# Eight-part query stack, two queues for the maxima, and fp32 dense experts beside five sparse ones in a two-layer attention and mixture kernel

## Chip, cores and metric

One NeuronCore of a Trainium2 chip. The metric is the device time of one execution in microseconds, median of the runs; lower is better. The kernel of before runs at 333.51 us (three runs, 332.26 to 333.8).

## What is computed

1024 tokens of 128 features pass through two layers, each an attention over a context of 96 features and a mixture of experts, all with a normalisation in front and a residual behind:

```python
x = x + L0_xattn(layernorm(x), ctx)     # one head, 4 batches of 256
x = x + L0_ffn(layernorm(x))            # 64 experts, top 6, plus a shared expert
x = x + L1_xattn(layernorm(x), ctx)     # 16 heads of 8, softmax(q k / sqrt 8) v, Wo
x = x + L1_ffn(layernorm(x))            # the last mixture:
    probs = softmax(xt @ Wr);  topv, topi = top_k(probs, 2);  topv /= sum(topv)
    rank = cumsum(onehot(topi), axis=0);  keep = (rank <= 160) * onehot
    w = einsum('tk,tke->te', topv, keep)
    h = gelu(xt @ W1[e] + b1[e]);  y = h @ W2[e] + b2[e];  out = sum_e w[t,e] * y
```

The last mixture has 8 experts of 512 hidden units and a capacity of 160 tokens for each of the two choices.

## The kernel before

It is written in one program per engine, with semaphores; the order on each engine is the order of the code. The first attention and the first mixture (up to 148 us of the span) stay as they are but for details. Then:

**Query stack.** The queries and keys of the second attention are split into three bf16 parts. Eight products of parts (PARTS_Q, PARTS_K) make up one fp32-like product, so each head has 64 stacked rows (KROWS) and three rows of maxima above them. `queries` (L1692, DVE), `query_parts` (L830, ACT), `query_residual` and `query_last` (DVE) make the parts of a batch; for batches 2 and 3 the DVE steps stand in the slots 0 to 4 of the loop below. `queries_stacked` (L463, the SP queue) writes the three parts to DRAM (parts 0 and 1 in one DMA once both exist, then part 2), waits for both writes and loads them back in three DMAs, rows 0 to 23, 24 to 47 and 48 to 63, all 16 heads. POOL clears the stack's upper half beforehand in `query_zeros` (L623): batch 3, then, after the last expert group, batches 0 to 2.

**Attention loop.** All engines walk SLOTS (L856, L1416, L1858). In slot s, PE makes the scores of maximum m = s (`max_scores`, L922 with ks as its second operand), DVE reduces them to the negated maximum (L1863), and PE makes the transposed scores of exponential e = s - LAG (`exp_scores`), for which ACT takes Exp (L879). LAG is 17. After each eight maxima POOL splits them into three bf16 parts (`maxima_parts`), PE transposes them in slot 8k+10, ACT copies them in slot 8k+11 (L862), and SP sends three rows of each half-batch into the query stack (`maxima_stacked`, L484). `exp_scores` waits for them at every eighth head. The division, output product and residual of each token chunk have fixed slots (TAIL_AT, TAIL_LAST), and so have the normalisation and router of each half of the tokens (STATISTICS to ROUTER_WT): steps 48 to 63 for the first half, 68 to 76 for the second.

**Router.** Logits, subtraction of the maximum (DVE), Exp (ACT), the two largest and their indices (DVE), ranks by matmul (PE), then in `router_weights` the slots of the dispatched rows and the weights as three bf16 parts. POOL's `dispatch_rows` scatters the tokens to DRAM in eight indirect DMAs for each half (L671), SP loads them back expert by expert (`dispatched_rows`, L498), PE transposes them (L1388).

**Last mixture.** Experts 3 to 6 are sparse (320 rows each), experts 0, 1, 2 and 7 dense, in two halves of 512 tokens. QS gives the order: six dense half rounds, four sparse rounds, two dense half rounds, each of four steps (NF). A step is `ffn_hidden(n)`, three fp32r matmuls on weights and inputs split into high and low (`split_weights` on POOL, L661 and L662; `operands` on DVE), Gelu twice on ACT (L903 as fp32r, L907 as fp32), the difference on DVE (L1915), and `ffn_out(n)` two steps later, three fp32r matmuls. Dense results are weighted by a broadcast row and summed into accT (L1806, L1854). Sparse results are biased, transposed (L1399), weighted (L1842) and scattered to DRAM by POOL (`return_rows`, L683), the last expert to a plane of its own.

**End.** SP loads the planes 0 and 1 of returned rows, POOL adds them to x (L711); plane 2 is loaded on two queues and added by DVE (L1940), as are the transposed sums (L1946), and x is stored in three chunks.

## Time and profile before

| | us |
|---|---|
| median of three runs | 333.51 |
| the profiled execution | 332.18 |
| its span | 330.4 |

| engine | busy us | share |
|---|---|---|
| PE matmul | 273.7 | 83% |
| DVE | 227.4 | 69% |
| ACT | 166.6 | 50% |
| POOL | 160.6 | 49% |

A busy time is the time in which the engine had an instruction in it; a matmul's includes the time until its result is written, so consecutive ones overlap and a group of n of them lasts n pitches and one latency. The granted clock is given as a share of 2.4 GHz: 1.00 is the upper of two levels, 0.50 (1.2 GHz) the lower. In an idle note as [2.27 <-DMA big<-q_parts] the engine had nothing to do for 2.27 us ahead of the instruction, and what came last was that DMA.

### The profile page before, as it was taken

Reading aid. Unit: us, or ns where it says so; the run is one execution under the profiler, and the core shown is the slowest. Engines: PE = TensorE matmul, PEld = TensorE weight load, DVE = VectorE, ACT = ScalarE, POOL = GpSimd, SP = SyncE. Lnnn points to the kernel's source line nnn. Section 1 sums busy time; section 2 is a strip of 40 time slices with the busy share of each in tenths; the row PEclk is TensorE's granted clock in tenths of the full one; section 3 lists DMA queues with packets and bytes.
Section 4 is the critical chain, followed back from the end, with each engine's and each line's share of the span. In section 5 each row is a group of like instructions: output and inputs, shape, how many; then the busy total and the mean of one; then the engine's idle time right before and its main releaser. Section 6 shows DMA issues by size and latency. Waiting matters only on the chain.

```text
span 330.4 us, 6098 instructions
## 1 busy us (share of the span) xinstructions
PE 273.7 (83%) x2180; PEld 187.6 (57%) x2180; DVE 227.4 (69%) x575; ACT 166.6 (50%) x323; POOL 160.6 (49%) x184
## 2 busy tenths in 40 slices
PE   1996766788989899987359999999898989899970
PEld 0665435367778778865112545554466667679740
DVE  2467889445675564437488777875648788999793
ACT  1455230342354235533232777778686978678830
POOL 5856373854234419426305433302271079977772
PEclk9999955999999999999755899999999999999995
DMA  6972294348996554230421500002300002500044
GB/s 205 305 258 100 63 189 76 41 40 212 207 195 163 147 149 34 86 107 1 111 66 37 128 18 4 1 3 87 110 15 4 0 21 57 165 0 12 27 139 128
DMA packets 22569, 30.66 MB, mean 93 GB/s; under 512 B 2926, under 2 KB 15135, under 8 KB 22283
## 3 DMA queue, kind: packets, MB, share of 16 engines
q1 hardware_dynamic: 19835, 26.46, 27.9%
q0 software_dynamic: 1920, 2.90, 8.0%
q10 hardware_dynamic: 784, 0.92, 0.9%
q8 instruction: 17, 0.28, 0.3%
q14 instruction: 13, 0.11, 0.1%
HBM read 23.19 MB, written 7.92 MB: 94 GB/s over the span
## 4 chain that ended last, share of the span: by engine, by line
PE 51%; DVE 17%; POOL 9%; issue 9%; DMA 7%; ACT 5%; DVEq 0%; SPq 0%; POOLq 0%; ACTq 0%
PE bank L922 43%; PE bank L1119 3%; POOL ew L616 2%; DVE score L1863 2%; POOL dispatched L671 2%; DMA packc<-in_packc 2%; DMA big<-q_parts 1%; DMA ew<-normalised,slot_token 1%; PE bank L1131 1%; ACT ctxT L796 1%; DMA returned_last<-ctxT,big 1%; POOL rstd L563 1%; POOL returned L683 1%; POOL big L626 1%; DMA ks<-returned_last 1%
## 5 line engine op out<-in xcount | busy, mean ns | idle before, releaser
L922 PE MATMUL bank<-frbuf,splits 128*128 128x512 f32 (+1 forms) x240 | 60.9, 388 | 2.0 <-DVE frbuf L1915 1.7
L616 POOL DMA_INDIRECT ew<-normalised,slot_token x32 | 33.1, 1036 | 43.7 <-DVE slot_token L1633 36.0
L1863 DVE TENSOR_REDUCE score<-bank 128x2 f32<-128x512 f32 x64 | 42.2, 687 | 14.4 <-PE bank L922 13.7
L922 PEld LDWEIGHTS bank<-frbuf,splits 128*128 128x128 f32 x240 | 41.9, 188 | 13.6 <-DVE frbuf L1915 3.9
L879 ACT ACTIVATE pbuf<-bank 128x512 f32<-128x512 f32 x64 | 37.1, 598 | 16.0 <-PE bank L922 15.6
L1915 DVE TENSOR_TENSOR frbuf<-pbuf,frbuf 128x512 fp32r<-128x512 f32 (+1 forms) x48 | 36.6, 775 | 5.6 <-ACT pbuf L907 5.1
L1639 DVE CAST splits<-bank 128x1024 fp32r<-128x1024 bf16 x16 | 19.6, 1223 | 25.8 <-PE bank L922 21.5
L903 ACT ACTIVATE frbuf<-bank,biases 128x512 fp32r<-128x512 f32 (+1 forms) x48 | 30.6, 638 | 11.0 <-PE bank L922 10.1
L922 PE MATMUL bank<-ks,big 128*128 128x256 bf16 x128 | 29.5, 323 | 6.4 <-DVE score L1863 3.7
L922 PE MATMUL bank<-splits,frbuf 128*128 128x512 f32 (+1 forms) x144 | 32.0, 373 | 0.8 <-ACT frbuf L824 0.8
L907 ACT ACTIVATE pbuf<-bank,biases 128x512 f32<-128x512 f32 (+1 forms) x48 | 30.3, 631 | 0.0
L671 POOL DMA_INDIRECT dispatched<-xn,didx x16 | 16.3, 1018 | 27.9 <-DVE xn L1784 23.6
L922 PEld LDWEIGHTS bank<-splits,frbuf 128*128 128x128 f32 x144 | 24.6, 188 | 5.1 <-ACT splits L802 1.0
L922 PE MATMUL bank<-big,ks 128*128 128x256 bf16 x128 | 25.3, 285 | 0.4 <-ACT pbuf L879 0.4
L796 ACT COPY ctxT<-bank 128x512 f32<-128x512 f32 x8 | 4.7, 585 | 41.2 <-PE bank L1069 41.2
L922 PEld LDWEIGHTS bank<-ks,big 128*128 128x128 bf16 x128 | 10.0, 106 | 25.1 <-DVE score L1863 13.3
L662 POOL TENSOR_TENSOR splits<-ew,splits 128x512 fp32r<-128x512 f32 x16 | 22.1, 1382 | 1.3
L646 POOL CAST nmp<-score 128x16 bf16<-128x16 f32 x8 | 1.6, 196 | 40.6 <-DVE score L1863 40.6
L802 ACT CAST splits<-bank 128x1024 fp32r<-128x1024 bf16 x16 | 16.2, 1014 | 6.9 <-PE bank L1119 6.9
L922 PE MATMUL bank<-pbuf,vaug 128*9 128x256 f32 x256 | 19.7, 381 | 0.0
L563 POOL TENSOR_TENSOR rstd<-veps,mhalf 128x4 f32<-128x4 f32 (+1 forms) x10 | 9.4, 944 | 18.6 <-DVE veps L1474 16.3
L922 PE MATMUL bank<-xnT,packa 128*88 128x512 f32 (+2 forms) x28 | 15.7, 685 | 1.5 <-ACT xnT L746 1.4
(222 smaller groups left out, 538.7 us busy)
## 6 DMA issues: line engine op xcount, KB each, us to landing
big<-in_w SPq DMA_DIRECT2D x8, 704.0 KB
ew<-in_ew SPq DMA_DIRECT2D x16, 256.0 KB, 3.5
big<-in_w SPq DMA_DIRECT2D x8, 352.0 KB
ks<-k_parts SPq DMA_DIRECT2D x4, 512.0 KB, 8.1
k_parts<-parts SPq DMA_DIRECT2D x2, 768.0 KB, 3.8
big<-q_parts SPq DMA_DIRECT2D x8, 192.0 KB
returned<-vbuf SPq DMA_DIRECT2D x1, 1024.0 KB, 15.2
ks<-returned SPq DMA_DIRECT2D x4, 256.0 KB, 3.7
```

The lines of the kernel that those rows point to most:

```text
L563: pool.tensor_tensor(out=rstd[:, cs], in0=veps[:, cs], in1=mhalf[:, 0:n], op=ALU.pow).then_inc(ln_rstd, 1)
L616: pool.indirect_dma_start(out=xg[:, g % 2, j, :], out_offset=None, in_=xn_dram, in_offset=bass.IndirectOffsetOnAxis(ap=slot_token[:, g % 3 ...
L662: pool.tensor_tensor(out=low, in0=ew[:, e % RING1, i, :], in1=high.bitcast(F32), op=ALU.subtract).then_inc(split, 1)
L671: pool.indirect_dma_start(out=disp_dram, in_=xn[:, c, :], in_offset=None, out_offset=bass.IndirectOffsetOnAxis(ap=didx[:, c, k:k + 1], axi ...
L802: a.copy(PTs[:, j, :], bank[4][:, :].bitcast(BF16)).then_inc(e_PTa, 1)
L879: a.activation(prob1[:, e % NPROB, :], bank[2 + e % 2][:, :], ACT.Exp).then_inc(a_exp, 1)
L903: a.activation(acth[:, n % NA, 0:w], bank[n % 3][:, 0:w], ACT.Gelu, bias=bias).then_inc(f_hi, 1)
L907: a.activation(act[:, n % 4, 0:w], bank[n % 3][:, 0:w], ACT.Gelu, bias=bias).then_inc(f_act, 1)
L922: return pe.matmul(out_, lhsT, rhs, start=start, stop=stop, skip_group_check=True)
L1639: v.tensor_copy(PTs[:, j, :], bank[3][:, :].bitcast(BF16)).then_inc(e_PTv, 1)
L1863: v.tensor_reduce(nm1[:, c, 2 * hp:2 * hp + 2], bank[m % 2][:, :].rearrange("p (h k) -> p h k", h=2), X, ALU.max, negate=True).then_inc(a_ ...
L1915: v.tensor_tensor(out=actl[:, n % NA, 0:w], in0=act[:, n % 4, 0:w], in1=acth[:, n % NA, 0:w].bitcast(F32), op=ALU.subtract).then_inc(f_lo, 1)
```

## The change

- PARTS_Q and PARTS_K change places, so the rows of one query part lie together: parts 0, 0, 0, 1, 1, 1, 2, 2. Each part is written to DRAM as often as it is used, on its own semaphore, and the stack is loaded in two DMAs (parts 0 and 1, part 2), for batch 0 in four, heads 0 to 7 first.
- Queries of batches 2 and 3: the first step goes to ACT with bias and scale, the two differences to POOL. One of POOL's clears moves ahead.
- Of the maxima's three rows SP sends two and ACT the third. LAG is 15.
- The router's softmax goes: the second weight over the first is e to the power of the difference of the logits, taken on POOL, the first is 1/(1 + that). Slots of rows are computed ahead of weights. The steps of norm and router stand earlier.
- Experts 2 to 6 are sparse, 0, 1 and 7 dense. Dense steps use unsplit fp32 weights and one Gelu, one matmul for hidden and one for out. POOL splits only sparse experts, into a ring of four. LOADS gives the order in which weights are loaded, from within the loop of the maxima.
- The rows dispatched are loaded ahead of the last expert's weights. DVE adds planes 0 and 1 ahead of the last weighted product; weighting and summing of the last halves take turns.

```diff
-PARTS_Q = (0, 1, 2, 0, 1, 2, 0, 1)
-PARTS_K = (0, 0, 0, 1, 1, 1, 2, 2)
+PARTS_Q = (0, 0, 0, 1, 1, 1, 2, 2)
+PARTS_K = (0, 1, 2, 0, 1, 2, 0, 1)
-LAG = 17
+LAG = 15
-TAIL_LAST = {6: dict(zip(TAIL_AT, (65, 65, 66, 66, 67, 67))),
-             7: dict(zip(TAIL_AT, (66, 66, 67, 67, 68, 68)))}
+TAIL_LAST = {6: dict(zip(TAIL_AT, (65, 65, 66, 66, 66.5, 66.5))),
+             7: dict(zip(TAIL_AT, (66, 66, 66.5, 66.5, 67, 67)))}
-STATISTICS, NORMALISE, NORM_T, NORMED, OPERANDS = (48, 68), (49, 70), (54, 70), (54, 70), (54, 71)
-ROUTER_LOGITS, ROUTER_SUB, ROUTER_EXP, ROUTER_CHOICES = (56, 72), (56, 72), (57, 73), (58, 73)
-ROUTER_RANKS, ROUTER_WEIGHTS, ROUTER_T, ROUTER_WT = (60, 74), (60, 75), (63, 76), (63, 76)
+STATISTICS, NORMALISE, NORM_T, NORMED = (48, 67), (49, 67), (52, 69), (52, 69)
+ROUTER_LOGITS, ROUTER_CHOICES, ROUTER_RANKS = (53, 69), (54, 69), (56, 70)
+ROUTER_SLOTS, ROUTER_WEIGHTS, ROUTER_T, ROUTER_WT = (56, 70), (57, 71), (59, 72), (59, 73)
-XT_FIRST, XT_AT, Y_AT, YT_AT, YS_AT = -2, -3, 5, 6, 6
+XT_FIRST, XT_AT, Y_AT, YT_AT, YS_AT = -1, -3, 5, 6, 6
-SPARSE = (3, 4, 5, 6)
+SPARSE = (2, 3, 4, 5, 6)
+LOADS = (2, 3, 4, 5, 0, 1, 6, 7)
+LOAD_AT = {3: 3, 4: 5, 5: 7}
+RINGW, NA = 4, 3
...
+        def maxima_row(queue, k, part):
+
+            queue.dma_start(qs[KROWS + part:KROWS + part + 1, k // 2, k % 2 * 8:k % 2 * 8 + 8, :],
+                            nmT[k % 2][part * 8:(part + 1) * 8, batch(k // 2)]
+                            ).then_inc(nm_in[k % 4], 16)
...
+                for part, done in enumerate((q1_hi, q1_mid, q1_lo)):
+                    sp.wait_ge(done, b + 1)
+                    at, n = PARTS_Q.index(part), PARTS_Q.count(part)
+                    sp.dma_start(qscratch[b, at:at + n].rearrange("i p t -> p i t"),
+                                 view(parts[:, part, batch(b)], (0, n), (1, TB))
+                                 ).then_inc(qd_out[part], 16)
+                for heads, done in (((slice(0, 8), qs_in[0]), (slice(8, NH), qs_in8)) if b == 0
+                                    else ((slice(0, NH), qs_in[b]),)):
+                    for at, end in ((0, low), (low, KROWS)):
+                        for part in range(2) if at == 0 else [2]:
+                            sp.wait_ge(qd_out[part], 16 * (b + 1))
+                        sp.dma_start(qs[at:end, b, heads, :], rows[at:end, heads, :]
+                                     ).then_inc(done, 16)
...
                 sp.wait_ge(a_nmT, k + 1)
-                for part in range(3):
+                for part in range(2):
+                    maxima_row(sp, k, part)
...
+            pool.wait_ge(e_Y, NG - 1)
+            query_zeros(0)
             pool.wait_ge(e_Y, NG)
-            for b in range(3):
-                query_zeros(b)
+            query_zeros(1)
+            query_zeros(2)
...
+            for b in (2, 3):
+                pool.wait_ge(q1_hi, b + 1)
+                pool.wait_ge(q1_res, b)
+                pool.tensor_tensor(out=query_rest(b), in0=qf[:, batch(b)], in1=parts[:, 0, batch(b)],
+                                   op=ALU.subtract).then_inc(q1_res, 1)
...
             for k in range(2 * NB):
                 maxima_parts(k)
-                if k < 2 * RING1:
-                    split_weights(k // 2, k % 2)
-            power(8)
+                if k == 2 * NB - 1:
+                    power(8)
+                    pool.wait_ge(ln_rstd, 9)
+                split_weights(SPARSE[k // 2], k % 2)
+            second_choices(0)
             dispatch_rows(0)
             power(9)
+            second_choices(1)
             dispatch_rows(1)
...
+                    a.wait_ge(a_nmT, k + 1)
+                    maxima_row(a, k, 2)
...
+                if h2 is not None:
+                    mm(o, expert_raw(e, 0)[:, chunk(f)], xnT[:, half(h2)]).then_inc(f_H, 1)
+                    return
...
+                if QS[q][1] is not None:
+                    pe.wait_ge(f_act, n + 1)
+                    mm(o, expert_raw(e, 1)[:, chunk(f)], act[:, n % 4, 0:w], start=(f == 0),
+                       stop=(f == NF - 1)).then_inc(f_Y, 1)
+                    return
...
+            v.wait_ge(x3_sb, NC)
+            for h2 in range(2):
+                returned_sum(h2, range(2))
             for at in (0, TB):
                 weighted(NQ - 1, at, TB)
-            for at in (0, TB):
                 summed(NQ - 1, at, TB)
-            returned_sum(0)
+            returned_sum(0, [2])
             layer_sum(0)
-            returned_sum(1)
+            returned_sum(1, [2])
             layer_sum(1)
             layer_sum(2)
```

## Rows read from the trace of the kernel before

**Rows 1.** First line of the profile page: the span.

```profile
span 330.4 us, 6098 instructions
```

**Rows 2.** Windows: us, busy of each engine (instructions), granted clock, DMA share, GB/s.

```profile
166.00:185.00 19.00, 15.28 (x63) 5.61 (x62) 16.60 (x29) 7.18 (x14) 5.28 (x12) 0.51 0.31 68
...
240.00:285.00 45.00, 41.33 (x216) 28.99 (x209) 35.15 (x91) 35.81 (x58) 24.66 (x23) 1.00 0.13 33
285.00:305.00 20.00, 19.22 (x116) 16.51 (x117) 19.30 (x38) 15.16 (x34) 15.73 (x15) 1.00 0.11 39
...
319.00:330.40 11.40, 1.85 (x8) 0.91 (x8) 5.84 (x9) 0.00 (x0) 5.17 (x4) 0.59 0.44 134
```

**Rows 3.** Timeline (start, us, engine, line), matmuls of 512 and 320 columns, one subtraction.

```profile
15.36 1.95 PE L922 MATMUL bank<-xnT,packa 128*128 128x512 f32 x4 [0.38 <-ACT xnT L746]
...
42.77 3.69 PE L922 MATMUL bank<-xnT,packa 128*88 128x512 f32 x4
...
273.73 5.73 PE L922 MATMUL bank<-frbuf,splits 128*128 128x512 f32 x24
...
300.32 0.49 DVE L1915 TENSOR_TENSOR frbuf<-pbuf,frbuf 128x320 fp32r<-128x320 f32 x1
...
300.65 0.60 PE L922 MATMUL bank<-xsT,splits 128*128 128x320 f32 x3
...
301.09 0.60 PE L922 MATMUL bank<-frbuf,splits 128*128 128x320 f32 x3
```

**Rows 4.** Groups by line and shape: count, busy us, mean ns, idle before.

```profile
L1915 DVE TENSOR_TENSOR frbuf<-pbuf,frbuf 128x320 fp32r<-128x320 f32 x16 | 12.3, 782 | 0.1
```

**Rows 5.** Timeline, from the first mixture to the first scores.

```profile
146.94 5.31 POOL L626 MEMSET big<- 64x2048 f32 x3 [11.14 <-PE bank L922]
...
160.03 1.11 SPq L475 DMA_DIRECT2D big<-q_parts  x3
...
165.72 1.01 PE L922 MATMUL bank<-ks,big 128*128 128x256 bf16 x4 [2.27 <-DMA big<-q_parts]
```

**Rows 6.** Timeline of the attention loop's slots.

```profile
166.34 0.69 DVE L1863 TENSOR_REDUCE score<-bank 128x2 f32<-128x512 f32 x1 [4.99 <-PE bank L922]
...
171.13 4.87 DVE L1863 TENSOR_REDUCE score<-bank 128x2 f32<-128x512 f32 x7
...
175.63 0.36 ACT L862 COPY ctxT<-bank 24x256 bf16<-24x256 bf16 x1 [4.24 <-PE bank L1230]
...
176.06 2.20 SPq L484 DMA_DIRECT2D big<-ctxT  x3
...
180.10 0.63 PE L922 MATMUL bank<-big,ks 128*128 128x256 bf16 x2
...
221.60 1.28 DVE L1863 TENSOR_REDUCE score<-bank 128x2 f32<-128x512 f32 x2
```

**Rows 7.** Timeline, from the first half's router to the first sparse step.

```profile
237.64 0.34 PE L1315 MATMUL bank<-identb,wparts 128*24 128x128 bf16 x3 [1.16 <-DVE wparts L1794]
...
238.79 0.93 PE L922 MATMUL bank<-frbuf,splits 128*128 128x512 f32 x3 [0.32 <-ACT ra L873]
...
257.47 1.28 ACT L869 ACT_TABLE_LOAD   x1
...
258.76 0.23 ACT L869 ACTIVATE sres<-sres 128x32 f32<-128x32 f32 x1
...
264.98 1.05 POOL L671 DMA_INDIRECT dispatched<-xn,didx  x1 [13.50 <-DVE xn L1784]
...
276.77 0.38 SPq L498 DMA_DIRECT2D big<-dispatched  x1
...
284.88 0.68 PE L922 MATMUL bank<-xsT,splits 128*128 128x320 f32 x3 [0.84 <-issue]
```

**Rows 8.** The chain of work that ended last (start, us, what), its last hops.

```profile
317.60 4.04 DMA returned_last<-ctxT,big
321.65 3.45 DMA ks<-returned_last
325.20 0.70 DVE x L1940
```

More of the change, by code:

```diff
@@ L430, in _ @@
                 sp.wait_ge(done, 2)
-                at, n = PARTS_K.index(part), PARTS_K.count(part)
-                sp.dma_start(kscratch[at:at + n].rearrange("i p t -> p i t"),
+                n = PARTS_K.count(part)
+                sp.dma_start(kscratch[part:NCOMB:3].rearrange("i p t -> p i t"),
                              view(parts[:, part, :], (0, n), (1, T))).then_inc(kd_out, 16)
@@ L641, in _ @@
                                op=ALU.add).then_inc(x2_sb, 1)
+            pool.wait_ge(x2_sb, NB + 1)
+            for b in (2, 3):
[3 more added lines that the diff above has]
+                                   op=ALU.subtract).then_inc(q1_res, 1)
+                pool.wait_ge(q1_mid, b + 1)
+                pool.wait_ge(q1_lo, b)
+                pool.tensor_tensor(out=parts[:, 2, batch(b)], in0=query_rest(b),
+                                   in1=parts[:, 1, batch(b)], op=ALU.subtract).then_inc(q1_lo, 1)
             def maxima_parts(k):
@@ L847, in _ @@
             norm_transposed(7)
+            for b in (2, 3):
+                a.wait_ge(q1_ps, b + 1)
+                a.wait_ge(q1_f, b)
+                a.activation(qf[:, batch(b)], bank[6 + b % 2][:, 0:TB], ACT.Identity,
+                             bias=bq1s[:, 0:1], scale=SCALE1).then_inc(q1_f, 1)
             query_parts(2)
@@ L1424, in _ @@
                 n = e - TILE0
[L1425 to L1436 removed]
+                for at in (e - 0.5, e):
+                    if at == e and 0 <= n < NT:
+                        ffn_hidden(n)
+                    for name in ("output", "normed transposes", "transposes"):
+                        c = tail_chunk(name, at)
+                        if c is not None:
+                            tail_steps[name](c)
+                    for h2 in range(2):
+                        if at == NORM_T[h2]:
+                            norm_transposes(8 + h2)
+                        if at == ROUTER_LOGITS[h2]:
+                            router_logits(h2)
+                        if at == ROUTER_RANKS[h2]:
+                            router_ranks(h2)
+                        if at == ROUTER_T[h2]:
+                            router_transposes(h2)
                 for hg in range(4 * NB):
@@ L1738, in router_less_maximum @@
                 v.wait_ge(r_ps, h2 + 1)
[L1739 to L1746 removed]
+                chained(v.tensor_copy(rp[:, cs, :], logits))
                 for c in range(first, first + 4):
```

316 lines of the change are left out of this document (141 added, 175 removed).

## Prediction

> **What bounds the kernel now.** Read the span first: 330.4 us [rows 1]; the execution took 332.18 us, so 1.8 us lie around the span, and it is 1.3 us under the median of 333.51. Then read busy time by stage [rows 2]. From 166 to 185 us the attention loop starts at a granted clock of 0.51 (the 1.2 GHz level) and DVE is busy 16.6 of 19 us. From 240 to 285 PE is busy 41.3 of 45 us, though 24 dense steps fill less (below). From 285 to 305 DVE (19.3 of 20) and PE (19.2) are level. In the last 11.4 us PE works 1.85 us: a pure chain of latencies. So PE sets most of the time, but four places wait: the start of the loop, the two routers, the sparse steps with their DVE subtractions, the end.
>
> **The dense mixture steps, removed and added.** Before, a dense step is six fp32r matmuls (three hidden, three out). 24 of them took 5.73 us; with some 0.25 us of latency off, 0.228 each, 1.37 us per step. After, it is two fp32 matmuls on unsplit weights. In the trace one fp32 matmul of 512 columns is two records: the two query projections are four records in 1.95 us, so 0.86 each with the latency off, 1.72 per step at 2.4 GHz; the same form at 1.2 GHz took 3.69 [rows 3]. Sparse steps keep six matmuls of 320 columns; groups of three start 0.44 us apart, 0.88 per step. Before 32 dense and 16 sparse steps: 43.8 + 14.1 = 57.9 us. After 24 and 20: 41.3 + 17.6 = 58.9. **PE work rises by 1.0 us.** What falls is elsewhere: one Gelu instead of two and no DVE subtraction in each dense step, no split of experts 0, 1 and 7 on POOL. The subtractions of 320 columns averaged 782 ns [rows 4], though the one at 300.32, with POOL only issuing DMAs, took 0.49 us [rows 3]. POOL now splits only one expert after the router. The fifth sparse expert adds its six transposes (two groups of about 0.5 us) and two half rounds less save two weight rows of 0.3: +0.4 us. I take 0.8 us off the stalls of the sparse stage, bounds 0 and 2.5 (all of DVE's excess, 20 x 0.3 = 6, cannot come back since PE was busy 19.2 of 20).
>
> **The head of the loop.** POOL's three clears of the query stack ran 5.31 us from 146.94 [rows 5], 1.8 each, ahead of POOL's part in the next norm; one now lies earlier, under the group before it. That gives about 0.8 us on the norm chain (bounds 0 and 1.8; DVE's own work before that norm hides the rest). The three stack loads were issued from 160.03 and the first scores began at 165.72 after 2.27 us of idle PE waiting for them, so the last projection had ended at 163.45. After, parts 0 and 1 are written on their own semaphores without waiting for each other, and the first loads carry only eight heads: half the bytes. I put the first scores where the last projection ends, 163.45 - 0.8 + 0.3 = 163.0: **-2.7 us** (bounds 0 and -3.0; beyond that PE itself is the bound). The larger writes (three and two copies of a part for one) are covered if they land within 3 us of their issue.
> The Trainium skill, "DMA: Bandwidth & Descriptors", section "Anatomy of one DMA", gives a DMA a fixed part of about 2.0 us plus bytes over 436 GB/s, mostly the write receipt; halving the bytes would by that save only 0.6 us on a load of the stack, and this part would be -1.4 with the 0.8 of the clears. The trace's 5.7 us from the first load's issue to the scores [rows 5] do not agree for loads of this size.
>
> **Slots 0 to 4.** DVE did queries, residual and last part of batches 2 and 3 (six operations) between the maxima: the first reduction began at 166.34 and the fifth at 171.13 [rows 6], 4.8 us for four intervals, where seven from there take 4.87, 0.695 each. The six go to ACT (idle then) and POOL (idle until the eighth maximum): 4.8 - 2.8 = **-2.0 us**, bounds -1.0 and -2.0. The cover: POOL must end its four subtractions before the eighth maximum, some 5.6 us after the first; if not, the first maxima parts come late.
>
> **Lag 15 for 17.** Two slots with maxima only (0.70 each) and two with exponentials only are traded for two mixed ones. From the first exponential scores at 180.10 to the last pair of reductions, ending 222.9, lie 47 mixed slots of 0.91; from there to 238.79 lie 17 of 0.94. So 2 x (0.70 + 0.94 - 0.91) = **-1.5 us** [rows 6, 7]. What pays for it is the wait on the maxima rows. Rows of half-batch k are copied in slot 8k+11 and wanted in 8k+15, four slots instead of six. Before, the copy at 175.63 is followed by three issues lasting 2.20 us, and the first exponential scores run at 180.10. Two rows on SP take about 1.4 us, the third goes on ACT's queue at the same time. From copy to landing I estimate 0.35 + 0.8 + 2.0 = 3.2 us (2.0 for the landing is an estimate: a write of rows of the returned planes took 4.0 [rows 8] and is the bound); four slots are 2.8 us at the start, 3.7 later. So 0.4 us at the first and near nothing at the seven others; ACT's own issue and its wait for the copy, some 0.7 us per half-batch, lie in ACT's idle time of mixed slots. Price taken **+0.8 us**, bounds 0 and +14 (with 4.0 us to land, 1.8 us late at each of eight). Queued behind ACT's wait are the exponentials of that slot.
>
> **Router, first half.** This is spread over steps 52 to 59 instead of 54 to 63. PE stood 1.2 us at its last transposes at 237.64, just before the first hidden step at 238.79 [rows 7]: **-1.2 us** (0 to -1.5).
>
> **From the first dense step to the sparse ones.** Before: 238.79 to 284.88, 46.1 us with 24 hidden and 22 out steps, 31.5 us of matmuls, so 14.6 of everything else [rows 7]. The table of exponentials was loaded again in the second half (1.28 us, and 1.28 for the way back), with the choices waiting. Now a power on POOL (an estimate of 1.0 to 1.5 us: POOL's power for the norm is the same form) stands in its place, beside the index search. Walking the new order by hand from the first hidden step: up to the last attention output four hidden steps, two out steps and about 2 us of transposes and head values, 7.2 us (the first out step also waits for table load and first Gelu); residual, statistics, power and normalisation 4.1, so the second half's norm stands at 11.3; transposes, copy and logits to 13.5; choices on DVE 2.3; ranks to 16.7; five small DVE operations give the slots at 18.3 us (before: POOL's first dispatch at 264.98, 26.2 us). Dispatch and loads take from 264.98 to 276.77 for the eight issues and landing, then 3.3 us of loads and 1.8 of transposes and split: rows ready at 35.2. PE reaches its first sparse step after 16 + 14 dense halves (25.8 us) and 8.7 of the rest: 34.5. I take 35.0. The rest falls from 14.6 to 35.0 - 25.8 = 9.2: **-5.4 us**, bounds -2 and -7.
> The Trainium skill, "ScalarE: Activation LUTs", section "What ACT_TABLE_LOAD costs", counts 2.66 us per switch with a drain behind the load. The trace does not show the drain: the exponential starts 1.29 us after the load does [rows 7]. By the page the gain would be up to 2.8 us larger.
>
> **The end.** The last rows went out at 317.60, behind returns held up by POOL's splits, landed 4.0 us later and were back at 325.20 [rows 8]; 5.2 us followed. After, POOL is free when the last sparse expert is weighted, six steps before the end, so its rows are in at about the time of the last out matmul. The chain is then PE's: last matmul, two halves weighted and summed in turn (2.2 us without POOL beside them), two additions and three layer sums (2.8), store (2.4): 7.4 us after the last matmul for 11.5 before: **-4.1 us** (bounds -2 and -5). The sums of the first two planes, four of 0.69 us, go from POOL to DVE ahead of the last expert; they fit while it waits for the last matmuls.
>
> **Sum.** -2.7 - 2.0 - 1.5 + 0.8 - 1.2 + 1.0 + 0.4 - 0.8 - 5.4 - 4.1 = -15.5 us. The profiled execution would be 316.7, the median 333.5 - 15.5 = 318.0.
>
> **Rivals.** *The waits move.* The dispatched rows, or the rows of maxima, become what is late: for it speaks that both margins above are under 1 us; against it, each is one chain. 2 us more at the sparse start and 0.6 us at each half-batch give 325. Chance 0.17.
> *PE at 1.2 GHz.* An fp32 matmul costs 0.85 us more at the low level [rows 3]. If the clock falls in the mixture and stays down for 18 of the 48 dense matmuls, all 15.5 us are gone; for all 48 it would be 359. Against it: the clock is 1.00 from 240 to 305 through stalls of over a microsecond [rows 2, 7], and PE is denser here than there. For it: PE waits about 2 us in pieces around the second norm. Slower, about 340, chance 0.05.
> *The moved work comes back.* POOL and ACT late at the head, the last expert's DVE sums late at the end: only the router and end parts count half, 328 to 332; chance 0.06.
> *More than told.* The sparse stage also gives its 2.5 and the end 5: 314; chance 0.08. The forecast itself: 0.64.
>
> **Numbers.** Likeliest 318.0. Forecast and the larger gain reach 312.5; the first rival reaches 326. Under 0.5% (about what a measurement of this kernel can tell from no change, 1.7 us) 0.04; slower 0.06; faster 0.90.
>
> **What would show it.** First scores near 163; reductions 0.7 us apart from the first; first exponential scores near 174, a DMA as the releaser there if rows are late; first dense hidden step near 232; dense steps 1.72 us apart with PE at 1.00; first sparse step 35 us later; last matmul near 308; PE idle under 8 us at the end. An idle stretch of PE ahead of a half-batch, or ahead of the first sparse step, with the maxima or dispatched rows as releaser, would make it wrong.

## The result, and the profile after

The changed kernel takes 330.36 us (median of 20 runs, 328.49 to 333.21), the kernel before 333.76 us in the 20 runs beside it: ratio 0.990, 95% interval 0.988 to 0.993. That is 3.4 us less, not 15.5, and outside the predicted range of 312.5 to 326. The profiled execution took 331.68 us with a span of 329.9 us, so again 1.8 us lie around the span.

The timeline at the places where one stage ends and the next begins (start, us, engine, line; L957 is the matmul helper, L922 before), after the change:

```profile
145.34 1.23 DVE L1687 CAST splits<-bank 128x1024 fp32r<-128x1024 bf16 x1 [2.95 <-PE bank L957]
...
161.51 1.72 SPq L502 DMA_DIRECT2D big<-q_parts  x4
...
165.56 1.01 PE L957 MATMUL bank<-ks,big 128*128 128x256 bf16 x4 [0.60 <-DMA big<-q_parts]
...
166.19 4.08 DVE L1903 TENSOR_REDUCE score<-bank 128x2 f32<-128x512 f32 x6 [3.32 <-PE bank L957]
...
176.59 0.60 PE L957 MATMUL bank<-big,ks 128*128 128x256 bf16 x2
...
245.06 1.12 PE L957 MATMUL bank<-xnT,ew 128*128 128x512 f32 x2
...
282.51 0.68 PE L957 MATMUL bank<-xsT,splits 128*128 128x320 f32 x3 [0.19 <-issue]
```

Three marks of before that the rows ahead of the prediction don't have (the cast late in the first mixture, the copy of the last maxima, and the first half's normalisation):

```profile
143.50 1.23 DVE L1639 CAST splits<-bank 128x1024 fp32r<-128x1024 bf16 x1 [2.95 <-PE bank L922]
...
225.19 0.35 ACT L862 COPY ctxT<-bank 24x256 bf16<-24x256 bf16 x1
...
227.04 1.11 DVE L1482 TENSOR_SCALAR xn<-x,mv,rstd 128x128 f32<-128x128 f32 x4 [1.15 <-POOL rstd L563]
```

With [rows 6, 7] these give the stages. "Predicted" is the stage of before with the terms of the sum that fall into it.

| stage, us | before | predicted | after |
|---|---|---|---|
| span's start to the cast | 143.50 | 143.5 | 145.34 |
| cast to first reduction (head) | 22.84 | 20.1 | 20.85 |
| to first exponential scores (maxima alone, two slots fewer) | 13.76 | 10.4 | 10.40 |
| to first dense hidden step (mixed slots, first half's router) | 58.69 | 58.2 | 68.47 |
| to first sparse hidden step | 46.09 | 35.0 | 37.45 |
| to the end | 45.52 | 47.7 | 47.39 |

The predicted stages add up to a span of 314.9 us, the measured ones to 329.9: 15.0 us too few. One stage holds two thirds of that, 10.3 us between the first exponential scores and the first dense step. The rest is 2.4 us in the stage behind it, 1.8 ahead of the cast (no part of the change, see the control) and 0.7 in the head. The 10.3 us are two things. First the slots. ACT copies the transposed maxima once in eight slots, so the distance of its copies is eight slots (timeline of ACT, after; first, second and last of eight copies):

```profile
173.47 0.36 ACT L899 COPY ctxT<-bank 24x256 bf16<-24x256 bf16 x1 [3.65 <-PE bank L1267]
180.72 0.35 ACT L899 COPY ctxT<-bank 24x256 bf16<-24x256 bf16 x1
...
227.28 0.35 ACT L899 COPY ctxT<-bank 24x256 bf16<-24x256 bf16 x1
```

(227.28 - 173.47) / 7 = 7.69 us, before (225.19 - 175.63) / 7 = 7.08 [rows 6]: 4.2 us over the seven intervals. Of these 0.4 are work that the prediction had counted: at lag 15 two of these slots are mixed that were maxima alone before, 2 x (0.91 - 0.70). So the slots cost 3.8 us where 0.8 was told. Then the first half's router. From the last copy to the first dense step 14 slots took 13.6 us before; the 12 left at lag 15 take 17.8, and 10.5 was told. The timeline around its normalisation after, and the windows behind it (us, busy of PE, PEld, DVE, ACT, POOL, granted clock, DMA share, GB/s):

```profile
227.84 2.57 DVE L1529 TENSOR_SCALAR xn<-x,mv,rstd 128x128 f32<-128x128 f32 x4 [1.15 <-POOL rstd L587]
227.87 0.61 POOL L697 CAST splits<-ew 128x512 fp32r<-128x512 f32 x1
228.56 1.26 POOL L698 TENSOR_TENSOR splits<-ew,splits 128x512 fp32r<-128x512 f32 x1
...
230.47 0.66 PE L986 MATMUL bank<-ident,xn 128*128 128x128 f32 x4 [2.84 <-DVE xn L1529]
```

```profile
228.00:230.00 2.00, 0.00 (x0) 0.00 (x0) 2.00 (x3) 0.00 (x0) 1.74 (x2) 1.00 0.03 6
230.00:232.00 2.00, 1.08 (x7) 0.79 (x8) 0.41 (x2) 0.84 (x2) 0.00 (x0) 0.96 0.92 248
232.00:234.00 2.00, 2.00 (x11) 1.94 (x12) 0.00 (x0) 1.22 (x3) 0.00 (x0) 0.50 0.80 277
...
238.00:240.00 2.00, 2.00 (x27) 1.05 (x25) 1.25 (x8) 1.84 (x4) 0.00 (x0) 0.83 0.02 4
```

DVE's four normalising operations take 2.57 us beside POOL's split of expert weights; before, with POOL idle, they took 1.11. PE waits 2.84 us for them, because the norm's transposes now stand two slots sooner behind the statistics in its order (52 for 54), ahead of scores that it could have made. Then the granted clock is at 0.50 (the 1.2 GHz level) for some 7 us. Before, it stayed at 1.00 through the same stretch, and from 224 to 237 us POOL did nothing but the power for the norm; its dispatches began at 237.15 (windows of before, the same columns):

```profile
224.00:232.00 8.00, 7.53 (x74) 3.93 (x73) 4.87 (x20) 6.17 (x13) 1.03 (x2) 1.00 0.38 122
232.00:240.00 8.00, 6.41 (x73) 3.22 (x75) 4.76 (x34) 5.09 (x11) 2.24 (x3) 1.00 0.24 82
```

The Trainium skill, "SBUF — State Buffer", section "SBUF: two separate sides", says that VectorE and GpSimd share a port pair under an exclusive lock: if VectorE's instruction is in a two-port mode, or has two SBUF inputs against a GpSimd one that reads SBUF, the one that starts first holds the pair for its whole length and the other blocks. The trace agrees as far as it goes: four operations that need 1.11 us alone end 1.46 us later beside two POOL operations of 1.87 us in all. No run shows in which mode the four ran.

What came as told: reductions 0.7 us apart from the first (4.08 us for six), and the end. The last matmuls of the hidden and output kind end at 322.96, 6.9 us before the span does (7.4 told). The timeline of the end, after:

```profile
320.22 2.74 PE L957 MATMUL bank<-pbuf,ew 128*128 128x512 f32 x6
...
323.06 0.48 DVE L1846 SCALAR_TENSOR_TENSOR qkbuf<-bank,biases,vbuf 128x256 f32<-128x256 f32 x1 [0.48 <-PE bank L957]
...
326.20 1.88 SPq L546 DMA_DIRECT2D out_x<-x  x3
```

The subtractions of the sparse steps, after (count, busy us, mean ns, idle before); in [rows 4] their mean was 782 ns:

```profile
L1950 DVE TENSOR_TENSOR frbuf<-pbuf,frbuf 128x320 fp32r<-128x320 f32 x20 | 10.7, 537 | 3.9 <-ACT pbuf L942 3.8
```

### The profile page after: what moved, and what is told of

It reads as the page before. It is cut to its first block, busy times and chain, and to the rows that moved or that the text cites. A ratio compares the mean times of both kernels' runs of the same rounds, so it can differ in the third digit from the quotient of the medians.

```text
span 329.9 us, 5865 instructions
## 1 busy us (share of the span) xinstructions
PE 279.3 (85%) x2112; PEld 176.1 (53%) x2112; DVE 200.1 (61%) x543; ACT 145.2 (44%) x290; POOL 147.3 (45%) x178
## 4 chain that ended last, share of the span: by engine, by line
PE 63%; DVE 15%; ACT 7%; DMA 6%; issue 4%; POOL 3%; ACTq 1%; DVEq 0%; POOLq 0%
PE bank L957 54%; DMA ew<-normalised,slot_token 3%; PE bank L1154 2%; DVE score L1903 2%; DVE xn L1529 2%; DMA packc<-in_packc 2%; ACT pbuf L914 1%; POOL rstd L587 1%; DVE pbuf L1661 1%; ACT ctxT L828 1%; PE bank L1311 1%; PE bank L1166 1%; DMA big<-q_parts 1%; PE bank L1104 1%; DVE st L1516 1%
## 5 line engine op out<-in xcount | busy, mean ns | idle before, releaser
L1903 DVE TENSOR_REDUCE score<-bank 128x2 f32<-128x512 f32 x64 | 41.8, 687 | 16.3 <-PE bank L957 15.5
L942 ACT ACTIVATE pbuf<-bank,biases 128x512 f32<-128x512 f32 (+1 forms) x44 | 26.8, 612 | 25.4 <-PE bank L957 25.4
L957 PE MATMUL bank<-splits,frbuf 128*128 128x512 f32 (+1 forms) x144 | 32.0, 373 | 0.8 <-ACT frbuf L856 0.8
L957 PE MATMUL bank<-ks,big 128*128 128x256 bf16 x128 | 29.0, 318 | 2.9 <-DVE score L1903 1.5
L957 PE MATMUL bank<-big,ks 128*128 128x256 bf16 x128 | 26.4, 292 | 1.8 <-ACT pbuf L914 1.6
L957 PEld LDWEIGHTS bank<-splits,frbuf 128*128 128x128 f32 x144 | 24.6, 188 | 5.1 <-ACT splits L834 1.0
L957 PE MATMUL bank<-pbuf,ew 128*128 128x512 f32 x48 | 26.1, 634 | 0.0
L957 PE MATMUL bank<-xnT,ew 128*128 128x512 f32 x48 | 25.2, 608 | 0.0
L957 PEld LDWEIGHTS bank<-ks,big 128*128 128x128 bf16 x128 | 9.5, 104 | 22.7 <-DVE score L1903 15.5
L957 PE MATMUL bank<-pbuf,vaug 128*9 128x256 f32 x256 | 20.6, 396 | 0.0
L957 PE MATMUL bank<-xnT,packa 128*88 128x512 f32 (+2 forms) x28 | 17.8, 768 | 1.5 <-ACT xnT L778 1.4
L957 PEld LDWEIGHTS bank<-big,ks 128*128 128x128 bf16 x128 | 11.0, 102 | 10.2 <-ACT pbuf L914 5.5
L726 POOL DMA_INDIRECT returned<-ctxT,big x12 | 12.0, 999 | 7.1 <-issue 4.0
L957 PE MATMUL bank<-frbuf,splits 128*128 128x320 f32 x60 | 13.4, 329 | 0.7 <-DVE frbuf L1950 0.7
```

Of the source, the lines that this page charges most:

```text
L726: pool.indirect_dma_start(out=yl_dram if last else y_dram, in_=yrow[0:n, j % 2, a, :], in_offset=None, out_offset=bass.IndirectOffsetOnAxi ...
L942: a.activation(act[:, n % 4, 0:w], bank[n % 3][:, 0:w], ACT.Gelu, bias=bias).then_inc(f_act, 1)
L957: return pe.matmul(out_, lhsT, rhs, start=start, stop=stop, skip_group_check=True)
L1903: v.tensor_reduce(nm1[:, c, 2 * hp:2 * hp + 2], bank[m % 2][:, :].rearrange("p (h k) -> p h k", h=2), X, ALU.max, negate=True).then_inc(a_ ...
```

## The experiments

The kernels stand in five groups (e to i), each run on one chip beside the kernel before. "Eight slots" is as above; "loop" is the stage from the first exponential scores to the first dense step, "second" the one from there to the first sparse step, all of the profiled execution. The kernels of the second group (f) are treated below, since their chip was unlike the others. The profiled execution of f2 is one of its two longest (342.48 us, its median is 340.53).

| kernel | ratio to before (95%) | eight slots | loop | second |
|---|---|---|---|---|
| e0_after | 0.986 (0.983 to 0.990) | 7.68 | 68.38 | 35.84 |
| e1_rows_on_sp | 0.987 (0.982 to 0.993) | 7.75 | 68.09 | 35.84 |
| e2_split_behind_router | 0.983 (0.978 to 0.989) | 7.66 | 65.71 | 37.48 |
| e3_router_late | 0.986 (0.982 to 0.989) | 7.66 | 66.97 | 37.54 |
| f1_lag17_rows_on_sp | 0.998 (0.994 to 1.002) | 7.05 | 63.90 | 42.76 |
| f2_lag17 | 0.996 (0.992 to 1.000) | 7.14 | 65.05 | 43.33 |
| f3_split_and_router53 | 1.001 (0.998 to 1.004) | 7.64 | 62.44 | 45.67 |
| f4_lag17_sp_split_router53 | 0.990 (0.986 to 0.994) | 7.06 | 59.54 | 45.77 |
| g0_after_again | 0.993 (0.989 to 0.997) | 7.63 | 67.99 | 35.85 |
| g1_head_values_copy_later | 0.993 (0.990 to 0.997) | 7.82 | 69.86 | 37.25 |
| g2_copy_split_router53 | 0.985 (0.982 to 0.989) | 7.78 | 65.77 | 38.62 |
| g4_lag17_sp_split_router53 | 0.976 (0.972 to 0.979) | 7.08 | 58.34 | 39.03 |
| h1_head_values_sooner | 0.993 (0.989 to 0.996) | 7.76 | 69.07 | 37.37 |
| h2_lag17_head_values_sooner | 0.982 (0.975 to 0.990) | 7.18 | 64.07 | 37.14 |
| h3_before_with_lag15 | 1.008 (1.005 to 1.011) | 7.67 | 62.41 | 46.65 |
| h4_head_values_split_router53 | 0.980 (0.974 to 0.987) | 7.75 | 62.98 | 38.70 |
| i1_lag16_sp_split_router53 | 0.978 (0.975 to 0.981) | 7.26 | 59.71 | 38.19 |
| i2_lag17_sp_split_router53 | 0.974 (0.969 to 0.978) | 7.05 | 59.54 | 38.91 |

**The control.** No edit.

> The changed kernel itself, beside the four others on the same chip: 328 to 333 us, a ratio to the kernel before of 0.985 to 0.995. In its profile I ask again for four places, to see which of them belong to the kernel: the first cast of the first mixture at 145.3 us (143.5 before), the copies of the maxima 0.97 us per slot apart, PE's wait of 2.8 us ahead of the norm's transposes near 230 us, and the granted clock of 0.50 from 233 to 239 us.

As told, in all four places. But the first of them doesn't belong to the kernel: the cast of the first mixture stands at 145.41 here, at 143.62 and 143.77 in two other kernels with the same code up to there (e1, e2), and at 145.35 in the kernel before with only its lag changed (h3). The 1.8 us ahead of the cast are no part of the change.

**Who issues the rows of maxima (e1, f2).** All three rows on SP:

```diff
-                for part in range(2):
+                for part in range(3):
                     maxima_row(sp, k, part)
...
-                    a.wait_ge(a_nmT, k + 1)
-                    maxima_row(a, k, 2)
```

> The changed kernel with all three rows of maxima on SP's queue and none on ACT's; the lag stays at 15. Theory A: what stretched the mixed slots from 0.89 to 0.97 us is ACT's own wait for its copy and its issue (0.37 + 0.64 us per half batch, ahead of exponentials that PE waits for). Then the slots go back to 0.89, 48 x 0.08 = 4 us less, the third row lands 0.7 us later than now and costs at most 1 us at the start: 326 to 329 us. Theory B: the rows themselves land late at a lag of 15, and SP's third issue makes that worse: up to 0.7 us more at each of seven half batches, 332 to 336 us, with PE idle ahead of the first exponential scores of a half batch and a DMA as releaser.

Neither theory alone: the slots didn't change (7.75 us), and the time didn't either. One wait took the other's place. In e0 PE waited 1.9 us for exponentials, 1.6 of it at four places behind ACT's issue (timeline of ACT and PE, e0, the longest of them); in e1 it waited 2.9 us for rows (timeline of PE, e1, its waits for rows):

```profile
181.18 0.64 ACTq L422 DMA_DIRECT2D big<-ctxT  x1
...
182.52 0.39 PE L957 MATMUL bank<-big,ks 128*128 128x256 bf16 x2 [0.85 <-ACT pbuf L914]
```

```profile
175.46 0.61 PE L955 MATMUL bank<-big,ks 128*128 128x256 bf16 x2 [0.51 <-DMA big<-ctxT]
...
183.10 0.39 PE L955 MATMUL bank<-big,ks 128*128 128x256 bf16 x2 [0.50 <-DMA big<-ctxT]
...
191.22 0.39 PE L955 MATMUL bank<-big,ks 128*128 128x256 bf16 x2 [0.99 <-DMA big<-ctxT]
...
207.46 0.39 PE L955 MATMUL bank<-big,ks 128*128 128x256 bf16 x2 [0.87 <-DMA big<-ctxT]
```

**The split of weights, and the router's place (e2, e3).** The split moved behind both dispatches; the first half's router at 54, 56, 56, 58, 58, 59, 62:

```diff
-                split_weights(SPARSE[k // 2], k % 2)
+                if k < 2 * NB - 1:
+                    split_weights(SPARSE[k // 2], k % 2)
...
             dispatch_rows(1)
+            split_weights(SPARSE[NB - 1], 1)
```

> The changed kernel with one of POOL's splits of expert weights (2 operations, 1.9 us) moved from just ahead of the first half's normalisation to behind both dispatches. Theory A: this split slows DVE's four normalising operations beside it (2.57 us for 1.11), so normalisation takes 1.1 us, PE waits 1.4 us in place of 2.8 ahead of the norm's transposes, and if the clock's fall comes from that idle, it stays up: 1.4 us less, up to 4 with the clock, 326 to 330. Theory B: DVE's operations are slow there for another reason or PE's wait is of the early place in the order: normalisation still takes over 2 us, or the wait comes back at the next step, 330 to 332.

> The changed kernel with the first half's norm transposes, logits, choices, ranks and weights put at slots 54, 56, 56, 58, 58, 59 and 62 as before the change or near it (52, 53, 54, 56, 56, 57 and 59 in the change). Theory A: the steps stood in PE's order before their inputs were ready; PE stood idle 2.8 us, the granted clock fell to 0.50 for some 6 us behind it, and logits and transposes cost 1 and 0.9 us more. Then idle and fall both go and 1.2 us of wait comes back at the last transposes: 3 to 4 us less, 327 to 329. Theory B: the clock falls at the same place whatever waits there (the stretch is thin in PE work in any case), and the gain is only the idle less what comes back: 330 to 332.

In e2 normalisation takes 1.11 us again, PE waits 1.38 instead of 2.85, the clock is low for 3 us instead of 7, and the loop stage gives 2.7 us (timeline of DVE and PE, e2):

```profile
226.14 1.11 DVE L1531 TENSOR_SCALAR xn<-x,mv,rstd 128x128 f32<-128x128 f32 x4 [1.15 <-POOL rstd L587]
227.31 0.66 PE L988 MATMUL bank<-ident,xn 128*128 128x128 f32 x4 [1.38 <-DVE xn L1531]
```

So the overlap with POOL is shown as the cause of the slow normalisation. The ratio of the whole kernel moved by 0.003 only, within both intervals, because 1.6 us came back: the second stage grew from 35.84 to 37.48, with the clock at 1.00. There the dispatched rows are loaded later. SP, too, works in order, and its program ahead of these loads says: wait until four sparse experts are split, load the last sparse expert's weights, wait for the dispatched rows. In e0 the fourth expert is split before the dispatches and those weights are issued from 230.06; in e2 the edit has put this split behind the dispatches, and SP stands until it ends. SP's waits in e2 (us in total, times, longest), then the timeline of POOL, SP and PE in e2, then of SP and POOL in e0:

```profile
SPq L438 <- POOL splits L698: 43.8, 1, 43.8
```

```profile
269.03 0.97 POOL L714 DMA_INDIRECT dispatched<-xn,didx  x1 [0.30 <-issue]
270.00 0.63 POOL L697 CAST splits<-ew 128x512 fp32r<-128x512 f32 x1
270.71 1.26 POOL L698 TENSOR_TENSOR splits<-ew,splits 128x512 fp32r<-128x512 f32 x1
...
272.00 0.33 SPq L438 DMA_DIRECT2D ew<-in_ew  x1
272.37 0.43 SPq L439 DMA_DIRECT2D ew<-in_ew  x1
272.85 0.43 SPq L525 DMA_DIRECT2D big<-dispatched  x1
...
276.56 0.64 PE L1433 MATMUL bank<-ident,big 128*128 128x128 f32 x3 [1.57 <-DMA big<-dispatched]
```

```profile
230.06 0.43 SPq L438 DMA_DIRECT2D ew<-in_ew  x1
...
273.33 0.97 POOL L714 DMA_INDIRECT dispatched<-xn,didx  x1 [0.30 <-issue]
...
275.58 0.38 SPq L525 DMA_DIRECT2D big<-dispatched  x1
```

From the end of the last dispatch to the load it is 2.85 us against 1.28: the split's end at 271.97 and two issues of weights stand in between. All eight kernels with the split moved have PE's wait for dispatched rows in front of the sparse steps (0.9 to 1.6 us) and SP's wait for the split, none of the others has either. So this is a side effect of the edit by way of SP's order. Loading the rows ahead of those weights would take it out; no run tried it.

In e3 the wait at the norm's transposes is gone and the loop stage gives 1.4 us, but two waits of 1.2 us stand elsewhere (exponentials at 228.8, choices at 236.9) and the clock falls twice: theory B, nearly. The time is e0's (329.23 us both).

**Lag 17, and all together (second group).** LAG = 17; router at 53, 54, 55, 57, 57, 58, 61 ("router53").

> The changed kernel with lag 17 and all three rows of maxima on SP's queue, as before the change. Eight slots (from copy to copy of the maxima) took 7.1 us before and 7.7 in the changed kernel, also with the rows on SP alone at lag 15, where PE waited 0.5 to 1.0 us for rows at four half batches. Theory A: lag 15 with either issuer costs the 0.6 us per eight slots, by ACT's issue or by rows late; at lag 17 from SP neither is left: 7.1 us per eight slots, the first exponential scores 1.4 us later, 2 x 0.9 us given back behind the loop: 4.2 - 1.5 = 2.7 us less, 326 to 327. Theory B: something else of the change slows the slots (larger loads of weights in them, POOL's splits in them): 7.7 us per eight slots stay, 330 to 332.

> The changed kernel with lag 17, the third row of maxima still on ACT's queue. This keeps ACT's wait and issue and takes away any lateness of the rows. Theory A1: ACT's 1.0 us per half batch is what stretches the slots: 7.6 us per eight slots, the 1.5 us of the lag lost on top, 330 to 332. Theory A2: the place of ACT's copy and issue among the attention output's steps counts, and it moves with the lag by two slots: 7.1 to 7.3 us per eight slots, 326 to 328. Theory B as for the run with the rows on SP: 7.7 us.

> The changed kernel with POOL's split behind the dispatches, and the first half's router one slot later than in the change (norm transposes 53, logits 54, choices 55, ranks and slots 57, weights 58, transposes 61). With the split moved alone, PE still waited 1.38 us for the normalised rows and 1.05 at the last transposes, and the granted clock fell for 3 us. Theory A: with both, no wait of over 0.7 us is left there, the clock stays at 1.00, and PE's first dense step comes 1.5 to 3 us earlier than with the split alone, 65.7 us behind the first exponential scores: 62.7 to 64.2, total 325 to 327. Theory B: the wait only changes its place and the clock falls again: 328 as with the split alone.

> All four edits together: lag 17, the rows on SP, the split behind the dispatches, the first half's router one slot later. If the loop's 0.6 us per eight slots and the router's waits are separate terms, their gains add: 7.1 us per eight slots, no fall of the clock, first dense step 58.7 + at most 1 us behind the first exponential scores (58.7 before the change, 68.4 in the changed kernel): 322 to 324. If they share a cause or one hides the other: 326.

On this chip the kernel before took 340.69 us, and all four traces have a stop that no trace of the other groups has: ACT, DVE and PE stand still together soon after the first dense step, and all that the profile gives as releaser is "remote". Their cast of the first mixture also stands some 4 us later (149.11 in f1). Timeline of ACT, f1:

```profile
246.95 0.60 ACT L912 ACTIVATE pbuf<-bank 128x512 f32<-128x512 f32 x1 [1.68 <-remote]
252.76 0.58 ACT L919 COPY qkbuf<-bank 128x512 f32<-128x512 f32 x1 [5.21 <-remote]
```

So no ratio of this group is compared with one of another. The loop stage lies ahead of the stop and repeats elsewhere: f4, g4 and i2, one kernel on three chips, have 59.54, 58.34 and 59.54. Eight slots are back at 7.05 us with lag 17 (theory A) and at 7.14 with ACT's issue left in: at lag 17 ACT's issue costs 0.09 us per eight slots, 0.6 us in all, so it isn't what stretches the slots by itself. Both router edits together give 5.9 us in the loop stage (68.4 to 62.4), more than 2.7 and 1.4: in f3 the clock doesn't fall there at all. Lag 17 with the rows on SP is worth 3.4 us of time at equal router (341.51 to 338.13). The gains nearly add, 8.8 us in f4 for 4.5 and 5.9 alone; in f4 the clock falls for some 3 us.

**Collisions in a slot (g1, g2, h1, h2, h4).** ACT's copy of the head values from 8o+12 to 8o+13 (g); PE's head values from 4hg+6+kc to 4hg+5+kc (h):

```diff
-                    if e == min(8 * o + 12, NB * NH):
+                    if e == min(8 * o + 13, NB * NH):
...
-                        if e == min(4 * hg + 6 + kc, NB * NH):
+                        if e == min(4 * hg + 5 + kc, NB * NH):
```

> The changed kernel again, so that the next three have it on their own chip. Where the kernel before takes 333.7 us, 328 to 331; where it takes 340.7, as on the chip of the last four runs, whose traces all have a stall of 5 to 7 us of ACT, DVE and PE together around 250 us, the same ratio of 0.986 if that stall is of the chip and alike in both kernels, about 1.00 if it lies heavier on the changed one.

> The changed kernel, where ACT copies the unnormalised head values of a half batch one slot later (13 instead of 12 slots behind its first exponentials). At lag 15 ACT's copy of the maxima, its wait, its DMA issue, one exponential and this copy of 0.58 us all stand in one slot; at lag 17 they stand two slots apart, and there ACT's issue cost only 0.1 us per eight slots. Theory C: that collision is what lag 15 costs. Then eight slots take 7.1 to 7.3 us in place of 7.7, and the time is 2.5 to 4 us less than that of the changed kernel beside it. Rival: what counts is that PE's transposes of the maxima meet the head values in one slot at lag 15 and not at 17, or that the rows are late: 7.6 to 7.7 us stay, and less than 0.5 us is gained.

> The same copy one slot later, POOL's split behind the dispatches and the first half's router one slot later, lag 15 with ACT's row as in the change. If the three terms are separate: first dense step 59 to 60 us behind the first exponential scores (68.4 in the changed kernel, 62.4 with the two router edits alone, 58.7 before), and 4 to 8 us less than the changed kernel beside it. If the collision theory is wrong: 62.4 us behind, and 3 to 4 us less.

> The kernel with lag 17, the rows on SP, the split behind the dispatches and the router one slot later once more, beside the changed kernel on its own chip. From the traces: against the changed kernel 9 us less between the first exponential scores and the first dense step, 1.3 us later at the first exponential scores, so up to 7 us less in all: a ratio to before of 0.965 to 0.975 where before takes 333.7. If rows or dispatch become what is late behind the first dense step, part of it is given back there, and it is 0.98.

> The changed kernel with PE's head values one slot sooner (5 and 6 slots behind a group's first exponentials, not 6 and 7). At lag 15 PE's transposes of the maxima stand in a slot that also has eight matmuls of head values; in the trace such a slot takes 1.41 us, one with head values alone 1.09, one without 0.69 (DVE's reduction), so the transposes cost 0.32 in the one and nothing in the other. Theory D: this meeting is most of what lag 15 costs. Then eight slots take 7.2 to 7.4 us instead of 7.65, and the kernel 2 to 3 us less than the changed one (ratio to before 0.980 to 0.987). Rival E: ACT's copy, wait and issue in the slot behind are the cost: 7.6 us stay. Rival F: head values one slot sooner wait for exponentials just issued: 7.7 us or more, PE idle with ACT as releaser.

> The mirror of it: the changed kernel at lag 17 with the rows on SP, head values one slot sooner. Now the transposes of the maxima meet the head values where at lag 17 they did not (eight slots took 7.05 us there, in two traces 7.06 and 7.08 with the router edits). Theory D: 7.3 to 7.5 us. Theories E and F: E has nothing of ACT's left here, so 7.05 to 7.1; F gives the rise of the run before here as well, with ACT as releaser.

> Head values one slot sooner, the split behind the dispatches and the first half's router one slot later, at lag 15 with the third row on ACT. If theory D holds and the terms add: first exponential scores 10.4 us behind the first reduction (11.8 at lag 17), first dense step 59 to 60.5 us behind them, ratio to before 0.972 to 0.978, like the best run so far (lag 17, rows on SP, same router edits: 0.9757). If it doesn't: 62 us behind them, 0.980 to 0.985.

Theory C fell: eight slots took 7.82 us, and the copy that was moved became what PE's transposes wait for (0.57 us twice). Theory D fell too: at lag 15, with the meeting gone, 7.76 us; at lag 17, with the meeting made, 7.18 and not 7.3 or more. The rival of D, new waits for exponentials just issued, doesn't hide a gain in h1: its listed waits of PE are 2.7 us for 2.3 in e0, 0.06 per eight slots. g2 and h4 gained from their router edits only, and not from the slots: 4.1 us of the loop stage in g2 beside g1, where a wait of 1.44 us and a fall of the clock are left, and 6.1 in h4 beside h1, where the clock stays up. g0 itself was slower than told, at 332.04 us. g4 came out at 0.976 beside its 0.993, just above the range told: the loop stage gave 9.6 us where 9 were told, but the second stage took 3.2 more (39.03 for 35.85), by the wait for rows and a fall of the clock.

**The lag alone (h3, i1, i2).** h3 is the kernel before with `LAG = 15`; i1 is g4 with `LAG = 16`; i2 is g4 again.

> The kernel before with lag 15 as its only change (three rows on SP). If the cost of lag 15 belongs to the lag and to the meeting on PE, and not to other parts of the change: eight slots take 7.6 to 7.8 us where they took 7.08, PE waits for rows at three or four half batches as in the run with the rows on SP, first exponential scores 1.4 us sooner, and the kernel is 1.5 to 3.5 us slower than before, ratio 1.005 to 1.010. If the other parts matter: 7.1 us, and the 1.5 us of the prediction come as a gain, ratio 0.996.

> The kernel with rows on SP, split behind the dispatches and router one slot later, at lag 16 in place of 17. If lateness of the rows is what lag 15 costs: rows have five slots (some 4.5 us) from copy to use, the waits for rows (2.9 us in all at lag 15) shrink to under 1 us, eight slots take 7.1 to 7.2 us, and the one slot saved gives 0.7 us: ratio 0.972 to 0.975. If alignment is: at lag 16 the transposes of the maxima stand in the first of the two slots with head values, at 15 in the second, at 17 in neither: 7.4 to 7.7 us per eight slots without a DMA as releaser, 1.5 to 3.5 us more: ratio 0.979 to 0.985.

> The control: lag 17, rows on SP, split behind the dispatches, router one slot later. Measured before at 0.9757 with four runs; I expect 0.974 to 0.980, eight slots in 7.06 to 7.08 us, and PE waits of 0.6 us in all between the first and the last copy of the maxima.

h3 settles whose cost it is: in the kernel before, with nothing else changed, lag 15 makes eight slots 7.67 us and the kernel 0.8% slower (timeline of ACT, h3, first and last copy):

```profile
177.41 0.36 ACT L862 COPY ctxT<-bank 24x256 bf16<-24x256 bf16 x1 [4.24 <-PE bank L1230]
...
231.12 0.35 ACT L862 COPY ctxT<-bank 24x256 bf16<-24x256 bf16 x1
```

Lag 16 lies near 17 (7.26 us), between the two theories of i1, and its time can't be told from i2's. Summed over the timeline between the first and the last copy, PE's listed waits are 0.6 us before and in g4, 1.2 at lag 16, 2.1 after, 2.4 in h3 (1.8 for rows, at two places) and 3.6 in e1 (2.9 for rows). With four slots of lead the rows from SP are late at two to four places, with five once by 0.4. With six they are never late in before, f2, g4, h2 and i2, and once in f1 and f4 (0.5 and 0.2).

## Why the prediction failed, point by point

- **Head, -2.7:** the step held, sized too high: -2.0. PE's wait for the stack is 0.60 us in place of 2.27 [rows 5]. That wait is nearly all of the 0.7 us missing. From the first load's issue (161.51) to the scores it is 4.05 us where it was 5.69 [rows 5], so smaller loads did help, but they were not covered: 192 KB took 3.3 us from issue to landing (list of DMAs from 158 to 170 us). The fit of the Trainium skill, "DMA: Bandwidth & Descriptors", section "Anatomy of one DMA", 2.0 us plus bytes over 436 GB/s, which the page gives for GpSimd's path and not for SP's queue, makes an estimate of 2.5 us of that load. The trace doesn't agree, and the -1.4 by that page was as far off as my -2.7.
- **Slots 0 to 4, -2.0, and two slots of maxima fewer, -1.4:** right to the tenth (13.76 to 10.40), and POOL and ACT were in time.
- **Lag, -1.5 + 0.8:** the first of two steps that failed. The gain of two slots came; the price was 3.8 us in the slots, not 0.8, so the lag cost about 2.3 us and gained nothing (h3: 2.9 us slower). I had the bound (0 to +14) and the mechanism (four slots of lead, ACT's wait with exponentials queued behind), and took a value near the lower end, saying that ACT's issue of 0.7 us lies in idle time. It doesn't at lag 15: on ACT's queue PE waits for the exponentials behind it, on SP's for the rows. But listed waits beyond those of before account only for 1.4 of the 3.8 us (after), and for 2.9 of 4.2 in e1; the rest, 1.3 to 2.4 us, is open. Two collisions that would explain it were tried and are out. The weight loads (PEld) don't settle it either: between the first and the last copy they wait behind DVE's reductions for 10.2 us at 24 places after and 5.9 at 12 before, but also for 10.3 at 23 in h2, where eight slots take 7.18 us.
- **Router, first half, -1.2 (0 to -1.5):** the second step that failed, with the wrong sign, and the larger one: from the last copy 17.8 us where 13.6 - 1.9 (two slots fewer) - 1.2 = 10.5 was meant. I treated an earlier place in PE's order as a thing that can only help. PE works in order, so a step placed ahead of its input stops all behind it; and the order on POOL put a split exactly beside the normalisation. [rows 3, 4] had shown DVE's subtractions at 782 ns with POOL at work and at 0.49 us without, and I used it for the sparse steps alone. Moving split and router together took back 5.9 us in f3 (beside e0) and 6.1 in h4 (beside h1). Even there the 12 slots take 12.1 and 11.8 us, no less than 13.6 - 1.9. The -1.2 came in no run; the nearest is g4 with 13.25 us for 13.6 in its 14 slots.
- **The clock:** I gave it 0.05 as a rival in the dense steps, at 18 of 48 matmuls. It fell elsewhere: 7 us behind the 2.84 us stop, and in most traces some 3 us in the second half's router. The second stage is 35.84, 35.84 and 35.85 us where the clock stayed up (e0, e1, g0) and 37.14 to 37.54 where it fell (after, e3, g1, h1, h2), for the same work: 1.3 to 1.7 us. Even one kernel goes both ways: g4 stays at 1.00 behind its first norm, i2 falls for 3 us, and its loop stage is 1.2 us longer.
- **First dense to first sparse, -11.1 in all (46.1 to 35.0):** within 0.9 us where the clock stayed up (35.84), 2.4 short in the profile after, 1.6 of it the clock. The power in place of the table of exponentials worked as told; the removed table load isn't isolated by any run.
- **PE's work, the extra expert, stalls, end (+2.2):** right as a sum, +1.9. No run separates its terms. The last matmul's end is 6.9 us ahead of the span's for 7.4 told.
- **The rivals:** "the waits move" named the maxima rows, at 0.6 us for each half batch, with a chance of 0.17. The size was near the price of the loop (3.8 / 7), but by luck: in the profile after, PE waits for no row, and rows are late by more than 0.5 us only with all three on SP at lag 15 (e1, h3). With the router's 7 us on top, which no rival had, its 325 would have been 332. Lag and router are two failures and not one: the stop at the norm's transposes is there at lag 17, too (3.03 us in f1), and at lag 15 with the router of before there is none (h3).

## What to carry to other kernels

When a lag or a lead is shortened, price each transfer at its slot, from both issuers, before counting the slots that are saved: here lag 17 with all rows on one queue beat lag 15 in both kernels. Before a step is moved earlier in an in-order engine's program, find when its input is ready and what other engines do in that moment; a stop of the matrix engine costs its length and, where the clock falls behind it, more: 1.2 us behind a stop of 1.25 (i2 beside g4). And before a step is moved later, find who waits for it in another engine's order, as SP did for the split. The best kernel found keeps the change but for lag 17, rows on SP, the split moved and the router one slot later: 0.976 and 0.974 of before in two groups, 325.7 us against 334, and 0.990 on the chip of the second group.

## What the runs showed of the hardware

- Four DVE operations took 2.57 us beside POOL's tensor operations (after, e0, f1) and 1.11 without (before, e2, f3, g4). 128x320 subtractions had a mean of 782 ns before and 537 after, where POOL splits only one expert beside them; no run isolates that.
- In the first half's router the granted clock fell to 0.50 behind stops of PE of 1.20 to 3.5 us, for 3 to 10 us, and not behind stops of 1.01 to 1.16 us (i1, h4, f3, before [rows 7], h3), nor behind one of 1.26 us (g4). In the second half's router it fell behind two short waits of 0.75 and 0.68 us in 12 of the 18 traces with the change, and not in 6. One and the same program showed both, at the first place (g4, i2) and at the second (after, e0).
- Rows written by POOL's indirect DMAs had landed 1.28 us after the last one's record ended: SP's first load, which waits for them, starts then (e0).
- On one chip PE stood still for 3.7 to 5.5 us in each of four traces, ACT and DVE with it, for no reason that the profile names (f1 to f4).
